# Two-stage early blocks across two quarters in a fused routed decoder layer

## The reference, cut to what matters

```python
# x (4, 256, 256); ids (4, 256); ctx_2048 (4, 256, 256) serves as Wg, Wu and Wd of the middle block
x = layernorm(x + attention(x, Wq, Wk, Wv, Wo))
# middle block: expert of a token from its id (known ahead), hidden size 256
y = ctx[e] applied to (silu(x @ ctx[e].T) * (x @ ctx[e].T))
x = layernorm(x + y)
# last block: expert from the data, 4 experts, d_ff 1024
logits = x @ Wr + br
probs = softmax(logits); top_w, top_idx = top_k(probs, 1)
h = silu(x @ Wg[top_idx]) * (x @ Wu[top_idx])
x = layernorm(x + top_w * (h @ Wd[top_idx]))
```

## Time and profile before

| | |
|---|---|
| median of 3 runs | 196.0 us (195.14 to 196.38) |
| profiled execution, own time | 197.44 us |
| its span | 195.3 us |
| mean granted clock of TensorE | 0.986 |
| TensorE busy | 176.0 us (90%) |
| VectorE, ScalarE, GpSimd busy | 126.8, 103.9, 112.0 us |
| moved by DMA | 29.14 MB |

### The profile page before, as it was taken

How to read it: one execution, slowest core, us unless ns; L and a number is a source line. 1 busy time by engine, 2 the same in 40 slices (tenths; PEclk the granted TensorE clock), 3 DMA queues, 4 the chain that set the end, 5 groups by cost and what they waited for, 6 DMA issues and landing times.

```text
span 195.3 us, 3893 instructions
## 1 busy us (share of the span) xinstructions
PE 176.0 (90%) x969; PEld 139.7 (72%) x969; DVE 126.8 (65%) x398; ACT 103.9 (53%) x274; POOL 112.0 (57%) x138
## 2 busy tenths in 40 slices
PE   1999997999999698989999999999999999999810
PEld 0877775357878463768888878888888888888610
DVE  3179987814678686745664374444799986888950
ACT  3136877535467837346773955653566522355530
POOL 7015366779826765446873068880588810277783
PEclk9999999999999999999999999999999999999995
DMA  5999999246998223044544305454040000011010
GB/s 154 361 342 419 378 363 313 90 142 174 313 365 352 86 88 89 22 124 130 193 157 134 138 0 163 162 163 166 0 143 21 0 0 3 0 54 57 23 62 24
DMA packets 15317, 29.14 MB, mean 149 GB/s; under 512 B 1726, under 2 KB 11968, under 8 KB 15170
## 3 DMA queue, kind: packets, MB, share of 16 engines
q1 hardware_dynamic: 13568, 25.68, 39.3%
q0 software_dynamic: 1440, 3.22, 4.7%
q10 hardware_dynamic: 290, 0.01, 0.1%
HBM read 20.41 MB, written 9.28 MB: 152 GB/s over the span
## 4 chain that ended last, share of the span: by engine, by line
PE 74%; POOL 10%; issue 7%; DMA 3%; DVE 2%; ACT 1%; another core or an unknown queue 1%; POOLq 1%; SPq 0%; DVEq 0%; ACTq 0%
PE bank L477 14%; PE bank L478 13%; PE bank L479 13%; POOL out_tokens L466 5%; PE bank L722 4%; PE bank L587 4%; PE bank L622 4%; PE bank L556 4%; PE bank L645 3%; PE bank L491 2%; POOL rstd L389 2%; PE bank L565 2%; PE bank L485 2%; PE bank L535 2%; DMA x_sorted<-buf,slot 2%
## 5 line engine op out<-in xcount | busy, mean ns | idle before, releaser
L385 POOL TENSOR_TENSOR w_lo<-stage,w_hi 128x512 fp32r<-128x512 f32 x48 | 61.3, 1301 | 43.8 <-ACT w_hi L796 43.8
L905 ACT ACTIVATE gate<-bank 128x256 f32<-128x256 f32 x44 | 17.0, 386 | 47.9 <-PE bank L479 44.6
L1194 DVE TENSOR_TENSOR hid<-bank,gate 128x256 f32<-128x256 f32 x44 | 18.7, 425 | 29.9 <-ACT gate L905 29.6
L477 PE MATMUL bank<-w_hi,xr 128*128 x88 | 35.9, 408 | 1.3 <-DVE xr L1157 0.8
L478 PE MATMUL bank<-w_lo,xr 128*128 x88 | 34.5, 392 | 0.0
L479 PE MATMUL bank<-w_hi,xr 128*128 x88 | 34.5, 392 | 0.0
L477 PE MATMUL bank<-w_hi,hT 128*128 x88 | 28.3, 322 | 0.7 <-DVE hT L1199 0.7
L796 ACT ACTIVATE w_hi<-stage 128x512 fp32r<-128x512 f32 x48 | 28.6, 630 | 0.3 <-PE bank L479 0.3
L478 PE MATMUL bank<-w_lo,hT 128*128 x88 | 24.7, 281 | 0.0
L479 PE MATMUL bank<-w_hi,hT 128*128 x88 | 24.7, 281 | 0.0
L477 PEld LDWEIGHTS bank<-w_hi,xr 128*128 128x128 f32 x88 | 16.6, 188 | 4.7 <-issue 2.5
(11 more groups left out here) (181 smaller groups left out, 324.2 us busy)
## 6 DMA issues: line engine op xcount, KB each, us to landing
stage<-in_w_ffn SPq DMA_DIRECT2D x16, 768.0 KB, 4.5
rows<-x_sorted SPq DMA_DIRECT2D x22, 132.0 KB, 2.3
x_sorted<-padrow SPq DMA_DIRECT2D x1, 2244.0 KB
x_sorted<-padrow SPq DMA_DIRECT2D x1, 2112.0 KB
buf<-in_x_tok SPq DMA_DIRECT2D x1, 1024.0 KB, 10.8
w_hi<-in_ctx SPq DMA_DIRECT2D x1, 1024.0 KB, 11.5
w_hi<-in_ctxT SPq DMA_DIRECT2D x1, 1024.0 KB, 14.1
x_sorted<-padrow SPq DMA_DIRECT2D x1, 792.0 KB, 12.6
```

Source lines behind the costliest of these rows:

```text
L385: g.tensor_tensor(out=lo, in0=src, in1=hi.bitcast(F32), op=ALU.subtract).then_inc(split_lo, 1)
L477: mm(dst, xhi, whi, start=start, stop=False)
L905: a(gate[:, (T + j) % 2, :], fA[j % 2][:, 0:FQ], ACT.Silu).then_inc(silu_done, 1)
L1194: v.tensor_tensor(out=hid[:, (T + j) % 2, :], in0=fA[j % 2][:, FQ:2 * FQ], in1=gate[:, (T + j) % 2, :], op=ALU.mult).then_inc(h_done, 1)
```

## The change

- **Stages.** The blocks of the last block's stage become known in three stages: blocks 0 and 1 after 5 tiles (`tables_a`), block 2 after 7 (`tables_b`), the rest after 11 (`tables_late`). SyncE waits per stage.
- **Items.** The first six items are quarters 0 and 1 of blocks 0, 1 and 2: (0,0) (0,1) (1,0) (1,1) (0,2) (1,2). Both quarters of such a block add up in one PSUM bank. Then quarter 0 and quarter 1 of blocks 3 to 10, then quarters 2 and 3 as before.
- **Weights of quarters 0 and 1** are loaded straight into the place of `w_lo` and split there, so the three `stage` buffers serve quarters 2 and 3 alone. The 12 pieces of quarter 1 are split before and in the middle block. VectorE takes the low part of 18 of the 36 pieces of quarters 0 to 2 (LO_BY_DVE). The pieces of quarter 2 start with item 14, two an item.
- **Places.** The context weights `ctx4` move from `w_hi` to the arena, over `xT`; their load waits for the last `z` product.
- **Pads.** All 33 blocks of pads are one DMA behind the `sorted_rows` and chunk 7.
- **Orders.** The loops of the middle block and of the first 14 items are written out for TensorE, ScalarE, VectorE and GpSimd. The `idle_products` (12, 6 and 3) between the two stages are gone. The exponential comes with item 15.

```diff
-LATE = T - EARLY
 SORTED = BATCH - 1
-ROUTED = 7
+STAGE_ENDS = (5, 7, T)
+STAGE_BLOCKS = ((0, 2), (2, 3), (3, T))
...
+EARLY_ITEMS = [(0, 0), (0, 1), (1, 0), (1, 1), (0, 2), (1, 2)]
+ITEMS = EARLY_ITEMS + [(q, t) for q in (0, 1) for t in range(3, T)] + [(q, t) for q in (2, 3) for t in range(T)]
+FIRST_ITEM = {q: next(j for j, x in enumerate(ITEMS) if x[0] == q) for q in range(NQ)}
+LAST_ITEM = {q: max(j for j, x in enumerate(ITEMS) if x[0] == q) for q in range(NQ)}
+WRITTEN_OUT = 14
+OPENS = (0, 1, 4)
+CLOSES = {2: 0, 3: 1, 5: 4}
...
+def reads_to(j):
+    return T + sum(i not in OPENS for i in range(j + 1))
+
+
+LO_BY_DVE = (4, 5, 6, 7, 8, 11, 12, 13, 14, 15, 17, 19, 20, 23, 26, 29, 32, 35)
...
+        def piece(n, i):
+            q, e = divmod(n, E)
+            o = ((q % 2) * E + e) * CHUNK + i * PIECE
+            lo = w_lo[:, o:o + PIECE]
+            src = lo.bitcast(F32) if n < 2 * E else stage[:, n % SLOTS, i * PIECE:(i + 1) * PIECE]
+            return n, i, src, w_hi[:, o:o + PIECE], lo
+
+        def in_chunks(a, b):
+            return [(n, i) for n in range(a, b) for i in range(PIECES)]
+
+        ORDER = (in_chunks(0, E) + [(n, i) for n in range(E, 2 * E) for i in range(PIECES - 1)]
+                 + [(n, PIECES - 1) for n in range(E, 2 * E)] + in_chunks(2 * E, NQ * E))
+        all_pieces = [piece(n, i) for n, i in ORDER]
         Q_PIECES = E * PIECES
-
+        GU_READY, DOWN_READY = Q_PIECES + E * (PIECES - 1), 2 * Q_PIECES
...
+        SHARE = {q: s for q, s in ((2, [2, 2, 2, 2, 2, 2]), (3, [0, 1, 1, 2, 1, 2, 1, 2, 1, 1, 0]))}
+        assert all(sum(s) == Q_PIECES for s in SHARE.values())
+
+        def pieces_in(j):
+            q = next((q for q in SHARE if 0 <= j - LAST_ITEM[q - 2] - 1 < len(SHARE[q])), None)
+            if q is None:
+                return ()
+            i = j - LAST_ITEM[q - 2] - 1
+            a = q * Q_PIECES + sum(SHARE[q][:i])
+            return range(a, a + SHARE[q][i])
...
+            def load_direct(n):
+                o = n * CHUNK
+                sp.dma_start(w_lo[:, o:o + CHUNK].bitcast(F32), wffn_in[n]).then_inc(d_direct[n], 16)
+
             def load_chunk(n):
-                if n >= SLOTS:
-                    sp.wait_ge(split_lo, pieces_to(n - SLOTS + 1))
+                if n >= 2 * E + SLOTS:
+                    wait_los(sp, (n - SLOTS + 1) * PIECES)
                 sp.dma_start(stage[:, n % SLOTS, :], wffn_in[n]).then_inc(d_chunk[n % SLOTS], 16)
...
-            load_chunk(1)
+            load_direct(1)
             sp.dma_start(ctxn, ctxn_in.rearrange("p (e k f) -> p e k f", e=E, k=DK)).then_inc(d_ctxn, 16)
-            load_chunk(2)
+            for n in range(2, E + 2):
+                load_direct(n)
+            sp.wait_ge(z_done, BATCH)
             sp.dma_start(ctx4[:, :, :, E:E + D], ctx_in.rearrange("p (e k d) -> p e k d", e=E, k=DK)).then_inc(d_ctx, 16)
-            load_chunk(3)
-            pads2 = scr2.rearrange("(p r) c -> p r c", p=P)
-            HALF2 = BLOCKS2 // 2
-            sp.dma_start(pads2[:, 0:HALF2, :], padrow[:].unsqueeze(1).broadcast_to([P, HALF2, ROW])).then_inc(d_init2, 16)
+            load_direct(E + 2)
...
-            sp.dma_start(pads2[:, HALF2:BLOCKS2, :],
-                         padrow[:].unsqueeze(1).broadcast_to([P, BLOCKS2 - HALF2, ROW])).then_inc(d_init2, 16)
-            for n in range(E, E + SLOTS):
+            load_direct(E + 3)
+            sp.dma_start(scr2.rearrange("(p r) c -> p r c", p=P),
+                         padrow[:].unsqueeze(1).broadcast_to([P, BLOCKS2, ROW])).then_inc(d_init2, 16)
+            for n in range(2 * E, 2 * E + SLOTS):
...
-            sp.wait_ge(row_table, 1)
-            r = [first_row(t) for t in range(EARLY)]
-            sp.wait_ge(d_scat2[0], 16 * ROUTED)
-            for t in range(EARLY):
-                routed_row(t, r[t])
-            sp.wait_ge(row_table, 2)
-            r = {t: first_row(t) for t in range(EARLY, EARLY + 2)}
-            sp.wait_ge(d_scat2[1], 16 * (T - ROUTED))
-            for t in range(EARLY, T):
-                if t not in r:
-                    r[t] = first_row(t)
-                routed_row(t, r[t])
-            for n in range(E + SLOTS, NQ * E):
+            for s, (a, b) in enumerate(STAGE_BLOCKS):
+                sp.wait_ge(row_table, s + 1)
+                r = {t: first_row(t) for t in range(a, min(b, a + 2))}
+                begin = STAGE_ENDS[s - 1] if s else 0
+                sp.wait_ge(d_scat2[s], 16 * (STAGE_ENDS[s] - begin))
+                for t in range(a, b):
+                    if t not in r:
+                        r[t] = first_row(t)
+                    routed_row(t, r[t])
...
+            split(9)
+            split(10)
             validity()
+            split(16)
+            split(18)
             root2(0)
+            split(21)
+            split(22)
             root2(1)
-            pool.wait_ge(d_init2, 32)
-            for t in range(0, 3):
-                scatter2(t)
+            pool.wait_ge(d_init2, 16)
+            scatter2(0)
+            scatter2(1)
+            scatter2(2)
+            scatter2(3)
             root2(2)
-            for t in range(3, ROUTED):
-                scatter2(t)
+            scatter2(4)
             root2(3)
+            scatter2(5)
+            scatter2(6)
             root2(4)
-            for t in range(ROUTED, T):
-                scatter2(t)
-
-            for q in range(NQ):
-                for t in range(T):
-                    if q < NQ - 1:
-                        for k in quarter_pieces(q + 1, t):
-                            split(k)
+            scatter2(7)
+            scatter2(8)
+            scatter2(9)
+            scatter2(10)
...
-            idle_products(12)
-            rank(3)
-            idle_products(6)
...
+            up(10)
+            th(9)
+            down(8)
+            th(10)
+            add(9)
+            rank(2)
+            down(9)
+            add(10)
+            down(10)
             ftx(0)
+            ftx(1)
+            fup(0)
+            rank(3)
+            fup(1)
+            fth(0)
+            fup(2)
             rank(4)
-            for i in range(len(items) + 2):
-                if i == EARLY:
+            fth(1)
+            ftx(2)
+            fdown(0)
+            fup(3)
+            fth(2)
+            fdown(1)
+            fup(4)
+            fth(3)
+            fdown(2)
+            fup(5)
+            fth(4)
+            ftx(3)
+            fdown(3)
+            ftx(4)
...
+                n, i, src, hi, _ = all_pieces[k]
+                q = n // E
+                if n < 2 * E:
+                    act.wait_ge(d_direct[n], 16)
+                    if q == 1 and i == PIECES - 1:
+                        act.wait_ge(mT_done, E // 2)
+                else:
+                    act.wait_ge(d_chunk[n % SLOTS], 16 * ((n - 2 * E) // SLOTS + 1))
+                    act.wait_ge(y_done, T + LAST_ITEM[q - 2] + 1)
...
+            for i in range(WRITTEN_OUT, len(items) + 4):
+                if i < len(items):
+                    fsilu(i)
+                if i <= len(items):
                     fhhi(i - 1)
...
+                for k in pieces_in(i):
+                    split(k)
+                if i == WRITTEN_OUT + 1:
                     a(lexp[:], rows[:, :, LOG:LOG + E], ACT.Exp).then_inc(lexp_done, 1)
...
+            def tables_a():
+                whole_blocks(T + 2, GROUP_OF[STAGE_ENDS[0] - 1] + 1)
+                running(nth[:], whole[:])
+                row_tables(*STAGE_BLOCKS[0])
+                chosen(0, 2)
+
+            def tables_b():
+                whole_blocks(T + 1, GROUP_OF[STAGE_ENDS[1] - 1] + 1)
+                not_taken()
+                running(nth[:], whole[:])
+                row_tables(*STAGE_BLOCKS[1])
+                chosen(1, 1)
+                step(v.tensor_tensor(out=flags[:, 0, :], in0=flags[:, 0, :], in1=flags[:, 1, :], op=ALU.add))
+
+            def tables_late():
+                dve.wait_ge(r_done, len(GROUPS))
                 step(v.tensor_tensor(out=by_expert(whole[:]), in0=per_block(pR[:, T, 0:E]), in1=begins[:], op=ALU.is_gt))
-                step(v.tensor_tensor(out=whole[:], in0=whole[:], in1=flags[:, 0, :], op=ALU.subtract))
+                not_taken()
                 running(nth[:], whole[:])
-                row_tables(EARLY, T)
+                row_tables(*STAGE_BLOCKS[2])
...
+            hidden(8)
+            residual(6)
+            place(1)
+            tables_a()
+            hidden(9)
+            hidden(10)
+            residual(7)
+            choose(2)
+            residual(8)
+            place(2)
+            tables_b()
+            residual(9)
+            fxlo(0)
+            choose(3)
+            fxlo(1)
+            residual(10)
+            split(23)
+            place(3)
+            fhidden(0)
+            choose(4)
+            fhidden(1)
+            fhlo(0)
+            place(4)
+            fhidden(2)
+            fxlo(2)
```

(2 more changed lines are left out.)

568 lines of the change are left out of this document (360 added, 208 removed).

## The result

The kernel after the change takes **209.1 us** (median of 4 runs, 207.83 to 212.16) against 196.2 us (4 runs, 195.14 to 196.55) for the kernel before on the same chip: ratio **1.062**, 95% interval 1.057 to 1.067. It is 12 to 13 us slower, and the range 193.2 to 200.4 does not hold it. The profiled execution took 208.01 us, with a span of 206.3 us against 195.3 and a mean granted clock of 0.969 against 0.986.

A forecast was written before the change was run, and what follows sets the result against it. TensorE is full from item 14, so time is set by when the last block's stage reaches this pace and by interruptions. Early gain -1.1 plus seam +2.8 gives +1.7 on the 196.0 median: 197.7 us, range 193.2 to 200.4.

The forecast's parts named there:

- The wait in item 14: Seam at item 14: ScalarE's first quarter 2 piece waits for item 13's fdown, with fsilu(15) and fhhi(14) queued behind.
- the forecast 3.4: Seam at item 14: fup(18) comes at X + 8.0 instead of X + 4.6, a loss of 3.4 us against 0.6 before.
- 50.0 + 1.9 + 12.7 = 64.6: Early stage: from 50.0 us chunk 7, then all pads, land by 64.6; the engines see it at 65.0, when scatter2(0) goes.
- The pads, 12.7 from 50.0: Early stage: all 4356 KB of pads (4.46 MB) at 350 GB/s take 12.7 us.
- The chunk, 1.9: Ahead of the pads: chunk 7, 768 KB at 420 GB/s, takes 1.9 us.
- The bounds 62.5 and 65.3: Pads' end in the early stage: 62.5 us at 420 GB/s, 65.3 at 340.
- I take 0: Quarter 1's splits before and in the middle block cost 0 us; at the upper bound for VectorE, up to 2 us.
- the wait for the pads hides that as well: Middle block: up to 2 us of delay from VectorE's low parts at the upper bound would be hidden.
- at pace: TensorE from item 14 on: 2.3 us an item; the seam's loss isn't made good.
- The clock: Rival, early seam: without idle products TensorE's clock falls, 1.5 us more, 199.2 us (up to 200.5); chance 0.22.
- Items 6 to 16: TensorE's stretch from fup(6) to fup(16): forecast 24.1 us, against 24.67 before.
- the worst case: Rival: middle block slows too, VectorE at the upper price and choose(0) late, 200.5 us and over; chance 0.06.

The follow-up runs named there:

- e5: Kernel before, with only all 33 pad blocks sent in one transfer behind the sorted rows' loads: ratio 1.0267 to the kernel before.
- e2: Changed kernel, no quarter 2 split in item 14, two in each of items 15 to 20, exponential in item 14: ratio 1.0403 to the kernel before.
- e4: Changed kernel with 20 products of ones ahead of rank(2) and four and four around ftx(1): ratio 1.0559 to the kernel before.
- e12: Changed kernel with only quarter 2's splits in items 14 to 19 set to 0, 3, 2, 3, 2, 2: ratio 1.0541 to the kernel before.
- e6: Changed kernel with chunk 7 loaded right behind chunk 6, ahead of the sorted rows' loads: ratio 1.0356 to the kernel before.
- e7: e1 with the low parts 7, 8 and 11 moved from VectorE to GpSimd: ratio 1.0388 to the kernel before.
- e1: Changed kernel with 16 pad blocks ahead of the context's load and 17 behind the rows: ratio 1.0383 to the kernel before.
- e8: e7 with 0, 3, 2, 3, 2, 2 splits in items 14 to 19 and the exponential in item 14: ratio 1.0196 to the kernel before.
- e9: e6 with e8's splits in items 14 to 19 and exponential in item 14: ratio 1.0189 to the kernel before.
- e13: e9 with items 5 to 13 written alike on TensorE, ScalarE and VectorE, one late block to an item: ratio 1.0301 to the kernel before.
- e15: e9 with the transposes of block j-1 in item j from item 6 on, copies likewise: ratio 1.0156 to the kernel before.
- e10: e9 with 8 of 33 pad blocks sent ahead of the context's load and 25 behind the rows: ratio 1.0166 to the kernel before.
- e11: e10 with e4's idle products: ratio 1.0293 to the kernel before.
- e14: e6 with the exponential moved to item 20 and the gates' weights to item 22: ratio 1.0207 to the kernel before.

## Why the prediction was wrong

**Right.** `scatter2(0)` waited for the pads, and `fup(0)` came later than before though two tiles fewer are waited for; e5 shows this alone. TensorE stood idle ahead of `rank(2)`, 5.25 us where some 4 were forecast, behind `root2(2)` and `choose(2)`. Items 0 to 6 took 13.74 us for 14.1. The wait in item 14 and the table loads were where the text put them: the two items concerned (3.76 and 4.66 us for 2.3 each) lose 3.8 us for the forecast 3.4.

**The step that failed first** is "50.0 + 1.9 + 12.7 = 64.6": the pads landed at 68.85, 4.25 us later. Two of its terms were too small.

- *The pads, 12.7 from 50.0.* In e5 no chunk stands ahead of them, so the sum gives 62.7; they landed at 64.82, 2.1 us later. The rate held (346 GB/s for 350), but the forecast gave the pads every byte from 50.0 on, and 0.67 of the 5.13 MB moved until they landed were not theirs. Which part of that was row loads not yet over and which the chunks behind isn't separated.
- *The chunk, 1.9.* It was priced at 420 GB/s, read where the queue held only chunks. From issue to landing the pads took 19.87 us behind it, and 19.02 to 19.75 in e2, e4 and e12, for 16.60 in e5: 2.4 to 3.3 us. Their issue also came 0.8 us later than in e5 (48.98 for 48.22). The page of before has 4.5 us from issue to landing for a chunk in the median; with the issue at 48.5 that alone would have put its end at 53.0, where it was in place at 55.4.

The bounds 62.5 and 65.3 varied only the rate, neither the start nor what shares the engines. At `scatter2(0)` the error is 4.7 us in the profiled execution (0.85 us lie between landing and scatter, for the 0.4 of the prediction), and 3.4 to 3.9 in the traces of e2, e4 and e12 (68.36 to 68.92 for 65.0). With the chunk elsewhere (e6) it is 1.6.

**"I take 0" for the splits that move.** The bound for VectorE's passes was right (six took 6.41 us for the forecast 4.1) and so was its being hidden (e7). What was not counted is ScalarE's wait for chunk 7 itself, which stopped TensorE for 1.50 us at 56.48. That "the wait for the pads hides that as well" holds for this one too as far as `fup(0)`: in e6 the wait is gone, and `fup(0)` comes no nearer to `scatter2(0)` (14.0 us for 13.8).

**The seam.** The 3.4 us of items 16 and 17 were nearly right (3.8), but "at pace" behind them was not. Of the 5.5 us that items 16 to 20 lose, 1.7 lie in item 18, which ran at a granted clock of 0.50. In e1 and e4, whose seam has the same code, the clock stays at 1.00 there, and items 16 to 20 still take 14.05 and 14.04 us: item 18 takes 2.6, and item 19 3.1, behind a wait of ScalarE for a weight chunk:

```profile
134.86 0.63 ACT L925 ACTIVATE w_hi<-stage 128x512 fp32r<-128x512 f32 x1 [2.13 <-DMA stage<-in_w_ffn]
```

With the fall (the changed kernel, e6 and e7) they take 14.58 to 14.74, so it is worth 0.5 to 0.7 us there. A likely reason why it isn't 1.7 is that the item at the lower clock gives that chunk time to come: in the changed kernel ScalarE waits 0.69 us for it. The other 1.1 us of items 18 and 19 are late copies of weights, which no step of the prediction had.

**The clock** was a rival with a chance of 0.22 and a price of 1.5 us. It did fall: at the early stage for 0.4 us at `ftx(0)` (e4), and at the seam, where no step had it, for the 0.5 to 0.7 us above. Where the pauses at the seam go (e2, e8, e9) it doesn't fall there, and items 16 to 20 come down by 5 us. The Trainium skill's "TensorE: Matmul & The Clock Gate" (Part 1) says that an idle array goes back to the throttled state; the early stage agrees, where the clock fell behind 5.25 us without a product. The seam doesn't settle it: no pause there is over 1.35 us, and e1 and e4 have nearly the same pauses without a fall. The forecast asked this only of the longest pause.

**Items 6 to 16** were taken "as before". They lost 1.5 us, or 2.1 where the 0.6 us of before's exponential is left out. The transposes of three more blocks lie in them (0.7 us); the other 1.4 us are waits. The new order writes `ftx(3)` and `ftx(4)` close ahead of `fup(6)`, which reads block 3 and waits for its copy on VectorE (97.27, above, at the end of item 5, which takes 3.13 us), and the same small waits stand in items 6, 8 and 11 (2.98, 3.32 and 2.84 us), where late blocks are transposed too. With a shorter lead in every item (e13) the loss grows, with a whole item of lead (e15) half of the waits go. The prediction priced only the arrival of blocks here, and not the copies behind the transposes.

**The range** held no sum of two bad cases. Pads and clock are not exclusive: a longer wait for the pads is a longer pause for the clock. They were given as single cases, and the worst case was left out of the range altogether.

**What stays open.** Why chunk 7 is so slow in that place: from 50 to 52 us e1 shows the same 170 GB/s, while e6, which has the pads there, shows 351. Why the clock fell at the seam in some traces and not in others. And the last 1.6 to 1.9% has no single cause: e9's span is 2.9 us over before's, 2.4 of it in items 4 to 13, of which 0.7 are three blocks' transposes that the kernel before has ahead of item 4 (0.24 us each), and 1.7 us waits. The other 0.5 us is a balance of small terms: -0.5 in items 13 to 16 and +0.6 in items 16 to 20, since the exponential's place moved, and +0.4 behind item 20, at 2.33 us an item for 2.31.

## What to carry to other kernels

When a transfer is moved behind others on a queue, price what stands between it and its new start by landing times in that place, not by the best rate seen elsewhere, and ask which engine waits for each of those. The bytes that share the engines with it count too. A saving of a few scatters is worth nothing if the buffer that they write is filled later. In a written order the distance from a producer to its reader is a quantity to keep: the same edits run at 2.55 us an item with one item of lead, and at 3.10 with 1.4 us of it.

## What the runs showed of the chip

- Behind pauses of TensorE that add up to 2.5 us of the seven from 125 to 132 us, no single one over 1.35 us, the granted clock was 0.50 and an item took 4.00 us. Behind nearly the same pauses it stayed at 1.00 in e1 and e4. In e1 and e10 pauses of at most 1.23 us ahead of item 0 came before a fall that took 1.3 us.
- One chunk of 768 KB issued behind eleven loads of 132 KB took 6.9 us to land (a wait for it ended 6.1 to 7.2 us behind its issue in e2, e4 and e12), where the median in the kernel before is 4.5.
- 4.46 MB of pads, with all the engines' traffic at 346 GB/s, landed 16.6 us after their issue (e5); by the rate alone they would need 12.9.
- Twenty idle products kept the clock at 1.00. They cost 2.5 us where the pause was 0.93 us without them (e11); where it was 5.25 us (e4) they brought `ftx(0)` 0.4 us nearer and showed no gain by item 6.
- Two function table loads of 1.28 us each cost 0.4 us on TensorE with no copies of weights among them (e9). With four copies about them, they and the fall of the clock behind them cost 3.8 (e6 against e14).
